# Layer normalisation of a two-layer decoder: the scaling moves from ScalarE to VectorE, GpSimd keeps only the power, and three input loads go to a second queue

## What is computed

```python
def _layernorm(x, axis=-1, eps=1e-05):
    m = jnp.mean(x, axis=axis, keepdims=True)
    v = jnp.var(x, axis=axis, keepdims=True)
    return (x - m) / jnp.sqrt(v + eps)
...
# layer 0: causal self-attention, 16 heads of 8
#          cross-attention on ctx, 8 heads of 64, with a bias
#          feed-forward with ternary weights and activations rounded to 8 bits
# layer 1: causal self-attention, 16 heads of 8, scores clipped to +-10
#          cross-attention on ctx, 16 heads of 64
#          mixture of 8 experts (gate, threshold 0.1, weighted sum)
```

## Time and profile before

| | us |
|---|---|
| three runs | 510.38, 511.57, 511.70 |
| median | 511.57 |
| the profiled execution | 509.18 |
| its span, from first to last instruction | 507.1 |

### The profile page before, as it was taken

One profiled execution on the slowest core, in us unless ns is written; L12 is line 12 of the kernel. 1 busy time (PEld: TensorE's weight loads), 2 busy tenths in 40 slices (PEclk: granted clock), 3 DMA queues, 4 the chain that ended last, 5 costly groups with the idle time before them and its releaser, 6 DMA issues.

```text
span 507.1 us, 15953 instructions
## 1 busy us (share of the span) xinstructions
PE 492.7 (97%) x5508; PEld 417.5 (82%) x5508; DVE 408.7 (81%) x939; ACT 437.1 (86%) x1177; POOL 390.3 (77%) x553
## 2 busy tenths in 40 slices
PE   7999999999999999999999999999999999999994
PEld 3888887888988888889888888888988888888882
DVE  4657778987888898889888898888888787866665
ACT  5989879999998888998798898989889998898761
POOL 3776777888967988888878977887888688685663
PEclk9999999999999999999999999999999999999999
DMA  5900000000000000000000000000000000000000
GB/s 168 352 4 2 3 1 3 1 3 2 3 2 7 2 8 2 1 2 14 0 3 7 3 7 2 2 6 3 8 6 2 3 6 3 7 1 8 1 12 10
DMA packets 6461, 8.65 MB, mean 17 GB/s; under 512 B 1392, under 2 KB 4848, under 8 KB 6384
## 3 DMA queue, kind: packets, MB, share of 16 engines
q1 hardware_dynamic: 6384, 7.65, 4.5%
HBM read 6.50 MB, written 1.05 MB: 15 GB/s over the span
## 4 chain that ended last, share of the span: by engine, by line
PE 63%; POOL 9%; ACT 7%; issue 7%; POOLq 6%; DVE 5%; DVEq 2%; ACTq 0%
PE psum L1179 9%; PE psum L1206 6%; PE psum L1166 6%; PE psum L1122 6%; PE psum L1234 6%; PE psum L1153 4%; POOL w_cross L695 4%; ACT w_cross L772 3%; POOL w_self L690 3%; POOLq L664 2%; PE psum L1245 2%; PE psum L1351 2%; PE psum L1192 2%; PE psum L1225 2%; PE psum L1217 2%
## 5 line engine op out<-in xcount | busy, mean ns | idle before, releaser
L690 POOL TENSOR_TENSOR w_self<-w_self 128x1024 f16<-128x1024 f32 x64 | 121.0, 1900 | 15.3 <-ACT w_self L761 7.6
L772 ACT ACTIVATE w_cross<-psum,row_max_cross 128x128 f32<-128x128 f32 x384 | 105.4, 415 | 7.0 <-DVE row_max_cross L913 6.9
L695 POOL TENSOR_TENSOR w_cross<-w_cross,e_rec_cross 128x1024 f32<-128x1024 f32 x48 | 90.9, 1899 | 16.3 <-DVE e_rec_cross L922 15.5
L913 DVE TENSOR_REDUCE row_max_cross<-psum 128x8 f32<-128x1024 f32 x48 | 58.0, 1215 | 12.3 <-PE psum L1166 12.0
L920 DVE TENSOR_REDUCE e_sum_cross<-w_cross 128x8 f32<-128x1024 f32 x48 | 58.3, 1214 | 4.3 <-ACT w_cross L772 4.1
L780 ACT ACTIVATE w_cross<-psum 128x1024 f32<-128x1024 f32 x48 | 50.2, 1053 | 5.7 <-PE psum L1179 5.2
L1166 PE MATMUL psum<-kT_cross,qT_cross 64*128 64x128 f32 x768 | 53.9, 283 | 0.0
L1206 PEld LDWEIGHTS psum<-w_cross,v_cross 128*64 128x64 f32 x768 | 41.1, 136 | 14.6 <-issue 12.1
L1206 PE MATMUL psum<-w_cross,v_cross 128*64 128x128 f32 x768 | 51.6, 278 | 0.6 <-issue 0.3
L1166 PEld LDWEIGHTS psum<-kT_cross,qT_cross 64*128 64x128 f32 x768 | 46.1, 187 | 7.0 <-issue 5.4
L1179 PE MATMUL psum<-ident,w_cross 128*128 128x128 f32 x384 | 49.3, 274 | 0.2 <-POOL w_cross L695 0.2
(11 more groups left out here) (198 smaller groups left out, 1405.7 us busy)
## 6 DMA issues: line engine op xcount, KB each, us to landing
out_dram<-x_all SPq DMA_DIRECT2D x16, 64.0 KB, 1.5
x_all<-in_x SPq DMA_DIRECT2D x1, 768.0 KB, 6.7
cT_all<-in_ctx SPq DMA_DIRECT2D x1, 768.0 KB, 8.6
e_k<-in_e_k SPq DMA_DIRECT2D x1, 512.0 KB, 4.4
e_v<-in_e_v SPq DMA_DIRECT2D x1, 512.0 KB, 5.3
e_q<-in_e_q SPq DMA_DIRECT2D x1, 512.0 KB, 8.3
e_o<-in_e_o SPq DMA_DIRECT2D x1, 512.0 KB, 9.1
m_w<-in_m_w SPq DMA_DIRECT2D x1, 512.0 KB, 8.6
```

Of the source, the lines that this page charges most:

```text
L690: pool.tensor_tensor(L.w_low[u], L.w[u][:], halves(L.w[u][:]), ALU.subtract)\
L695: pool.tensor_tensor(L.diff[u][:].rearrange("p (h k) -> p h k", h=UNIT), L.e[u][:].rearrange("p (h k) -> p h k", h=UNIT), L.e_rec[:, u, :] ...
L772: last = act.activation(L.e[u][:, P * p:P * (p + 1)], S_[:, P * p:P * (p + 1)], ACT.Exp, bias=L.row_max[:, u, p:p + 1])
L913: dve.tensor_reduce(L.row_max[:, u, :], group(i, turn)[:].rearrange("p (h k) -> p h k", h=UNIT), AX_X, ALU.max, negate=True).then_inc(L.ma ...
```

## The change

1. `rs` on POOL is now the power alone. The addition of epsilon is done on DVE, as a third instruction of `stats` (a drain and a tensor_scalar over one element per partition). The product minus mean times `rstd` is gone.
2. `nm` moves from ACT to DVE: one tensor_scalar over the 128x128 tile that subtracts the mean and multiplies by `rstd`, both read per partition.
3. `stats` now waits for `xn_ready` of the sequence before, instead of `rstd_ready`, because `nm` reads `mean_var`.
4. `c0`, `b_k` and `b_v` are loaded by three DMAs issued on ACT's queue, ahead of everything else on ACT. SP leaves them out and issues the mask copies right behind `x1`.
5. The table `ORDER` is new for all of PE, DVE, ACT and POOL, with new assumed costs (`rs` 640 for 1272, `nm` 270 on DVE for 380 on ACT, 100 more on each step that ends in `stats`). The instructions of all other steps are the same.

```diff
     def norm(L, source, users, read="xTe"):
-        add(f"{L}.rs", "POOL", 1272, [source], [f"{L}.nm"])
-        add(f"{L}.nm", "ACT", 380, [f"{L}.rs"], [f"{L}.un" if L == "ffn" else f"{L}.xT"])
+        add(f"{L}.rs", "POOL", 640, [source], [f"{L}.nm"])
+        add(f"{L}.nm", "DVE", 270, [f"{L}.rs"], [f"{L}.un" if L == "ffn" else f"{L}.xT"])
...
-        add(f"{L}.res", "DVE", 835, [f"{L}.y"], [f"{following}.rs"])
+        add(f"{L}.res", "DVE", 935, [f"{L}.y"], [f"{following}.nm"])
...
-        LOADS = dict(x0=[], first=["a_qk", "a_v"], x1=[], c0=[], b_k=["b_k"], b_v=["b_v"],
+        LOADS = dict(c0=[], b_k=["b_k"], b_v=["b_v"], x0=[], first=["a_qk", "a_v"], x1=[],
...
+        KEYS_VALUES_FIRST = ("c0", "b_k", "b_v")
...
             for group_name in LOADS:
+                if group_name in KEYS_VALUES_FIRST:
+                    continue
...
-                if group_name == "b_v":
+                if group_name == "x1":
                     sp.wait_ge(consts, N_CONSTS)
...
-                pool.tensor_tensor(L.var_eps[:], L.mean_var[:, 1:2], eps[:], ALU.add)
-                pool.drain()
-                pool.tensor_tensor(L.rstd[:], L.var_eps[:], minus_half[:], ALU.pow)
-                pool.drain()
-                pool.tensor_scalar(L.minus_mean[:], L.mean_var[:, 0:1], L.rstd[:], -1.0, ALU.mult, ALU.mult)\
-                    .then_inc(L.rstd_ready, 1)
+                pool.tensor_tensor(L.rstd[:], L.var_eps[:], minus_half[:], ALU.pow).then_inc(L.rstd_ready, 1)
...
-            def normalise(L, i):
-                act.wait_ge(L.rstd_ready, i + 1)
-                if i and L is not ffn:
-                    act.wait_ge(x_full, full(i - 1, f"{L.name}.xT"))
-                act.activation(L.xn[:], x_all[:, i, :], ACT.Identity, bias=L.minus_mean[:], scale=L.rstd[:])\
-                    .then_inc(L.xn_ready, 1)
...
+            act.dma_start(cT_all[:, 0:EARLY, :], t["ctx"][:, 0:EARLY, :]).then_inc(loaded["c0"], 16)
+            act.dma_start(wt["b_k"][:], t["b_k"]).then_inc(loaded["b_k"], 16)
+            act.dma_start(wt["b_v"][:], t["b_v"]).then_inc(loaded["b_v"], 16)
             act.wait_ge(consts, N_CONSTS)
...
             def stats(L, i, x):
                 if i:
-                    dve.wait_ge(L.rstd_ready, i)
+                    dve.wait_ge(L.xn_ready, i)
                 dve.bn_stats(L.moments[:], x)
                 dve.drain()
-                dve.bn_aggr(L.mean_var[:], L.moments[:]).then_inc(L.stats_ready, 1)
+                dve.bn_aggr(L.mean_var[:], L.moments[:])
+                dve.drain()
+                dve.tensor_scalar(L.var_eps[:], L.mean_var[:, 1:2], LN_EPS, None, ALU.add).then_inc(L.stats_ready, 1)
+
+            def normalise(L, i):
+                dve.wait_ge(L.rstd_ready, i + 1)
+                if i and L is not ffn:
+                    dve.wait_ge(x_full, full(i - 1, f"{L.name}.xT"))
+                if i and L is ffn:
+                    dve.wait_ge(units_ready, i)
+                dve.tensor_scalar(L.xn[:], x_all[:, i, :], L.mean_var[:, 0:1], L.rstd[:], ALU.subtract, ALU.mult)\
+                    .then_inc(L.xn_ready, 1)
```

More of the change, by code:

```diff
@@ L135, in cross_attention @@
         fill(f"{L}.y", 893 * chunks, [f"{L}.oTe.{c}" for c in range(chunks)], f"{L}.res")
-        add(f"{L}.res", "DVE", 840, [f"{L}.y", *biased], [f"{following}.rs"])
-    for name, cost in (("x0", 3000), ("first", 600), ("x1", 2300), ("c0", 400), ("b_k", 700), ("b_v", 1300),
-                       ("masks", 2000), ("more", 3300), ("e_k", 1400), ("e_v", 1500), ("x", 1900), ("ctx", 2400), ("self1", 800), ("cross1", 3900), ("moe", 1300)):
+        add(f"{L}.res", "DVE", 940, [f"{L}.y", *biased], [f"{following}.nm"])
+    for name, cost in (("x0", 2950), ("c0", 750), ("first", 400), ("b_k", 500), ("b_v", 900), ("x1", 500),
+                       ("masks", 3100), ("more", 3000), ("e_k", 1400), ("e_v", 1500), ("x", 1900), ("ctx", 2400), ("self1", 800), ("cross1", 3900), ("moe", 1300)):
         add(f"in.{name}", "SP", cost, once=True)
@@ L147, in all_steps @@
         add(f"{name}.lo", engine, lo, [f"{name}.hi"], once=True)
-    add("self0.st", "DVE", 440, ["in.x0", "consts", since("in.x1", 1), since("in.x", EARLY)], ["self0.rs"])
+    add("self0.st", "DVE", 540, ["in.x0", "consts", since("in.x1", 1), since("in.x", EARLY)], ["self0.nm"])
     self_attention("self0", "self0.st", True, "cross0", "in.first", "in.more")
@@ L156, in all_steps @@
     fill("ffn.y", 56, ["ffn.xTe", "tern.make"], "ffn.res")
-    add("ffn.res", "DVE", 875, ["ffn.y"], ["self1.rs"])
+    add("ffn.res", "DVE", 975, ["ffn.y"], ["self1.nm"])
     self_attention("self1", "ffn.res", False, "cross1", "in.self1", "in.self1")
@@ new lines @@
+        "bea1aUa6a6bWa4aXaLaOaHaZbWbabjbcaUbla1aQaJbebnb2aXbYaOaZaLa6a1bab2bwbcaHa4bja4byaUbeblaQb2bCbnaJbEbG"
+        "baaXbcaLbJaZa4aHbja1bebwbla6byb2a4bQaObaa6bSbnbCbYbEbGaUbUbjbcaQbJblbebwb6a6b8bybncca4aXcaaLbQbCaJaZ"
+        "bEclbGbSaHa1bUbja4chbJblcjb6bwcqb8babycaccclbncsbQaObCbca6b0bSb2aQaJbUbEcubYaUbwbechb6cqbycaaXbJcsaZ"
+        "aLa4cyb8bGa1clcccBcjcCcubQcGbjaHaOb0cya6aJblb2aUcKbCbnbScBbaaQbUbEbcchbebGb6bJb8cCcqcaaXbwcGcsclccaZ"
+        "bQcjb2aLbya1bScubUbjbWbWaHaOblbCaJbabnb0bGcyaUbccqcBcKbEaQcCchbebJb6cjcsbwcGcaaXb8byclccaLaZa4a1cubW"
@@ L227 @@
[L227 removed]
+        "aqaIasauaMaKa7a7a7a7a5awaRaIa5a5ayaVa5bXbZaKbZbZaAbXa0aMb1b1b1bXaIaVaRaKa7b1bZb1b3bbaMaIa0aCbdbXaRaK"
+        "aVbga7bXaMa7a5aIa0bbbkbdaVbXbmaRaKbgbZb3bva0aMa7bbb3bda5aIbka5aVbmaRbDbgbbb3bFbHaKaMbda0bvaIbLbkbOa5"
+        "bgbma5a7b3bba7bTbDbZbHbFaVbkaRbdbvbmbLb7bOa7b9bga5cecbbDaMaKbFa0bHbTcnaIa5bkcibvbmckb7bOb9bLcbcrcebb"
+        "ctcnbDbdb1a7bTb3aRaKbvbFbZaVb7cicrbgcbbLa0aMa5czb9bHctbOcEckcecncHaIbkczb1a7aKbmb3aVbDbTbbcEbFbdaRci"
@@ new lines @@
+        "bsa3a3b4aWaSbMbAbPbibscgaNa8b4a3cpbPbIbAbMbscgaFaSb4cpaWcwbMbia8bIbPbAaNcwcgcJaWbsb4cpbIaSbMbPa3cJbi"
+        "bAa8a3cwcpcgb4bsaFbIaSaNaWcJbPbMbAbicwa8cpaFaNcgbIbsaSaWb4a3bPbMaFbia8bAcJcwb4cpaSbscgaWaNa3cJbIbPbi"
+        "bAbMa8aNcwaFcpcgbsa3aWb4aSaFcJbPbibMbIbAa3cwa8aNcgb4bsaScpbIaWbibMbPaNbAcwcJa8cgcpaFa3bsbIb4aSaWcJbP"
+        "bicwa8bMaNbAcpcgaWbsaSb4cJbiaSaNa8bIaWbAcwa3cpbMa8bPbscgbib4a3cJbPbIcwbAbMbicgbsa3cpb4cJbIbsbMbPbAcw"
+        "cgb4cpbIcJbAbPbMcgcwb4bIcpbMbPb4cpcgcwcJcgcpcwcJcwcJcJ"
@@ L807, in do_step @@
                     high_copy(name.partition(".")[0])
-                if step == "nm":
-                    normalise(L, i)
                 if step == "un":
@@ L1062, in do_step @@
                         dve.tensor_copy(ident_b[:], ident[:]).then_inc(const_b, 1)
+                if step == "nm":
+                    normalise(L, i)
                 if step == "qz":
```

75 lines of the change are left out of this document (30 added, 45 removed).

## The result

| | us |
|---|---|
| before, median | 511.63 (510.38 to 511.77) |
| the changed kernel, median of four | 568.45 (567.31 to 569.66) |
| ratio | 1.1129, 95% interval 1.1108 to 1.115 |
| span of the profiled execution | 565.4 (before 507.1) |

The change costs 56.8 us.

What follows compares the result with a forecast made beforehand. PE and DVE's nearly full queue were taken to share the limit in the middle. +38.4 (100 to 450 us), +5.4 (50 to 100) and -0.3 (start) made +43.5 on 509.2: 553 us, range 509 to 572.

Steps and rivals of the forecast that it cites:

- That DVE's queue decides: DVE, at 98% of its full level from 200 to 250 us, gets 0.85 us more per normalisation and sets the time.
- POOL's relief: Busy time falling by some 44 us on POOL, and 51 on ACT, without effect on the time.
- The scaling undisturbed: The moved scaling on DVE (L886) without blocking: minimum near 0.29 us, 0.21 us of DVE's queue.
- Blocking, 0.40 per scaling: Each scaling on DVE waits for a POOL instruction already running: 0.40 us on average, bounds 0.15 and 0.65.
- The room of 21.1 + 4.8 us: Work DVE could still take up free: 21.1 us from 100 to 450 us, 4.8 from 50 to 100.
- the gain at the start: A shorter path of the normalisation at the start, while PE is still in warm-up matmuls: at most 0.3 us gained.
- The sum without blocking, 519: Rival A: no blocking, 0.44 us remain per normalisation and DVE's queue still bounds; 519 us, 514 to 528, chance 0.15.
- The granted clock: PE's clock, 1.00 in the first 50 us with PE busy 46.14 of 50: nothing added for it.
- Loads 0 ±1: Three DMA issues on ACT's queue and earlier masks: 0 us, bounds -1 and +1.
- Start and end: 0: Added DVE work of 6.8 us (first 50 us) and 5.1 (last 57) fits the room there: 0; start -0.3.
- Rivals B and C: B: DVE finds room, PE alone bounds, 505 us, chance 0.17. C: cost and gains cancel, 509 to 513, chance 0.08.

Runs made afterwards that it cites:

- small_pool_after: The changed kernel with POOL's two large instructions cut from 128x1024 to 128x2, leaving out part of the computation: 527.66 us, ratio 1.0337.
- accum_after: The changed kernel with the scaling on DVE also writing a sum, which does not write the same tile: 532.08 us, ratio 1.043.

## Why the prediction was right in its sign and short in its size

**That DVE's queue decides: right.** L886 has the range of durations that was forecast but for its minimum, DVE waits 1.4 us from 200 to 250, and the chain went from PE to DVE. PE, which before waited no more than 0.2 us at any place from 100 to 450 us, has waits like these there (the same view as for DVE above):

```profile
PE psum L1184 <- DVE w_self L934: 4.7, 7, 2.0
PE psum L1211 <- ACT qT_cross L735: 3.1, 1, 3.1
PE psum L1158 <- DVE weighted L1012: 2.7, 2, 2.0
PE psum L1356 <- DVE xn_self L886: 1.9, 2, 1.6
```

The tiles that PE waits for are mostly those of DVE's other steps, pushed back by the scalings ahead of them in the queue. POOL's relief was forecast well (44 us, measured 41.1), ACT's not (51, measured 28.8): I added up the 0.55 us of each activation, but neighbours on ACT overlap, so one taken out of the row frees less (without the 96, the others in the trace of the kernel before cover 408.0 us of its 437.1). It changes nothing in the sum.

**The scaling undisturbed, "near 0.29": 0.33 to 0.34.** The step reads two scalars per partition, and the sum charged 0.06 us for one; with two it would have been 0.35. Some 4 us in all.

**Blocking, 0.40 per scaling: 0.41.** Right, and for the stated reason, with both factors: the share of starts within a large instruction was put at 0.385, and it is 37 of 96, 0.385; the wait there was put at 0.95 us, and it is 0.98. A tensor_scalar from SBUF to SBUF that begins within a long instruction of POOL ends 0.08 us behind it (or when its own 0.34 us are over, where that is later). Two words of the forecast go too far. It is not any instruction of POOL: the power over one column holds nothing up. And "nothing done" can't be, since the step ends 0.08 us behind POOL and takes 0.34 alone; what the traces show is that it does not end before. The Trainium skill, "SBUF — State Buffer", section "Who interferes with whom", says of the ops that grab the pair shared with GpSimd that tensor_scalar is one, "not the form that also writes out its accumulator", and that an instruction with one SBUF input outside the 2-port modes doesn't contend. The runs agree: of the 58 plain scalings that began within a POOL instruction all 37 under the large ones ended behind them, and the 57 of the accumulating form and the 62 statistics that began within one were not held up. (That a BATCH_NORM_STATS2 is outside the 2-port modes the section does not say; it only doesn't name it among those that can enter them.)

**The room of 21.1 + 4.8 us: this step failed.** Counted from the trace (busy, plus gaps up to 0.15 us, plus longer waits), DVE stands before at 408.7 + 38.7 + 57.7 and after at 487.8 + 44.2 + 31.3. So its queue grew by 84.6 us, where 96 x 0.85 = 81.6 was forecast: 3 us. Its waits shrank by 26.4, where the forecast let 81.6 - 43.8 = 37.8 be taken up: 11.4 us. The two together are the 14.4 by which the span's growth, 58.3 from 507.1 to 565.4, exceeds the 43.8 of the sum before the gain at the start. By stretch, DVE's longer waits shrank like this:

| | before | after | taken up | forecast |
|---|---|---|---|---|
| first 50 us | 16.8 | 10.4 | 6.4 | 6.8 |
| 50 to 100 us | 5.5 | 2.7 | 2.8 | 4.8 |
| from 100 us to the last 57 | 21.3 | 7.4 | 13.9 | 21.1 |
| last 57 us | 14.1 | 10.7 | 3.4 | 5.1 |

So the room in the middle was measured rightly (21.1 us against 21.3 of waits), but only two thirds of it could be used, and that is half of the error.

The runs that add little to DVE show the same more sharply. Epsilon on DVE added 20.0 us of queue and 10.8 of time; a spare BATCH_NORM_STATS2 added 13.8 and 7.4. (The queue is from the traces, the time from the medians. The traced executions themselves are 14.5 and 9.2 us longer than that of the kernel before. PE has the same order in all three, and comparing them matmul by matmul, 2.8 and 1.4 us of this arise in the first 20 us, where these two executions have 6.8 and 3.4 us at half the clock and that of the kernel before has none.) I had treated DVE's waits as a pool that fills first, so that the first 21 us are free. In a fixed order they are not: by the medians 54% of either addition arrives at the end. The likely reason, argued from the way the rows are laid out and not tested by itself, is that each wait sits at one place of DVE's row, and work added elsewhere moves the tiles that PE waits for. In the changed kernel 26 of 85 us were absorbed. And the share is not a constant: in the new order with the scaling on ACT epsilon on DVE cost nothing.

**The sum without blocking, 519: 528 to 532.** The same error seen from the other side. Of the 57 us, 36 to 41 are the collision (82 x 0.40 = 33 in my sum) and 17 to 21 are queue and order (10 in my sum). The range held the result in part by luck: its top stood for a blocking of 0.65, and the result came near it with a blocking of 0.41.

**The granted clock, "I add nothing": wrong, by an estimated 6 us.** PE's busy time grew by 21 us over the same matmuls. In the profiled execution of the kernel before the clock is full until the last 1.2 us; in that of the changed one there are stretches like these (windows view, columns as above):

```profile
218.70:220.70 2.00, 0.19 (x4) 0.22 (x8) 1.93 (x4) 0.00 (x0) 1.86 (x4) 0.95 0.00 0
220.70:224.10 3.40, 3.40 (x21) 1.67 (x23) 3.32 (x5) 1.00 (x5) 3.15 (x3) 0.53 0.00 0
224.10:227.50 3.40, 3.40 (x68) 3.22 (x65) 2.99 (x5) 3.23 (x10) 1.78 (x3) 1.00 0.02 5
242.50:244.50 2.00, 0.04 (x1) 0.04 (x1) 1.93 (x3) 1.27 (x6) 1.86 (x3) 0.97 0.00 0
244.50:247.90 3.40, 3.40 (x17) 3.40 (x18) 2.71 (x4) 1.03 (x1) 0.36 (x1) 0.51 0.00 0
```

PE sat idle for 2 us (first for `weighted` of DVE's L1012, then for `w_self` of its L934), and then 3.4 us follow in which the granted clock is about half: almost all of it at the lower of the two levels, 1.2 GHz and not 2.4. 21 matmuls run there and 68, of other shapes, in the next 3.4 us. Five such stretches, at 8.9, 53.3, 220.5, 244.4 and 322.9 us, lie ahead of the program's end; the profiled execution of the kernel before has none ahead of its end, and neither have those of `small_pool_after` and `accum_after`. PE has the same order in these two as in the changed kernel, so the same matmul can be compared: across each of the five stretches the changed kernel falls behind either of them by 1.0 to 1.5 us, 6.4 in all. Taken as what the clock costs this is an estimate, and rather an upper one; it lies within the 36 to 41 us of the collision: PE idles because DVE is late, and then runs slowly.

**Loads 0 ±1: +1.** Right. **Start and end: 0.** DVE took up the additions there nearly as forecast (table above); the 0.3 us gained at the start were not measured by themselves. **Rivals B and C** needed DVE to find room; it found less than I gave it.

**What stays open.** Why the new order costs the old normalisation just 34 us, step by step; whether an order laid out with the measured 0.34 us for `nm` and with POOL's large steps kept away from it would come near the kernel before; and a form of the scaling that computes the right tile and is not held up. None of the three was tried.

## What to carry to other kernels

Before a tensor_scalar from SBUF to SBUF goes to VectorE, look at what GpSimd does: its price on VectorE's queue is its undisturbed duration plus the share of the time that GpSimd is within long instructions times half of such an instruction, here 0.34 + 0.41 us for an operation that looks like 0.3. The waits of an engine in a hand-fitted order are no free room: here half of each of two small additions was in the time at once. Count on the order to be worth as much as the change (here some 30 us in 510), so that a change of place is only tested together with an order made for it. A control that cuts the suspect (GpSimd's long instructions) in both kernels tells in two runs whether it is the collision or the load.

## What the hardware showed that I had not expected

- The accumulating form of the tensor_scalar takes 0.40 us and 0.08 for its second instruction, and is never held up by POOL, in 57 overlaps; the plain one takes 0.34, and has a mean of 1.02 in its 58 overlaps.
- What holds the plain form up are POOL's wide instructions (128x1024 for 1.9 us); under POOL's power over one column (0.55 us) it takes its 0.33 to 0.34 and ends first, four times in the changed kernel.
- A tensor_scalar over 128x128 from SBUF to SBUF takes 0.23 us with fixed scalars (L1040) and 0.33 with two read per partition; with the spare tile's two it takes 0.32.
- A second BATCH_NORM_STATS2 over the same tile takes 0.26 us where the first takes 0.29.
- Five times in the changed kernel PE's clock was granted at half for 3.4 us, each time behind a wait of PE (0.8 to 2.1 us), and each time that cost an estimated 1.0 to 1.5 us more, so a late tile of DVE can cost PE more than its lateness.
